# One wait of TensorE for free banks and for operands, where both stand on the same semaphore

## The reference

```python
x = x + attn(layernorm(x))            # Nystrom attention: 16 heads of 16, 64 landmarks
x = x + xattn(layernorm(x), ctx)      # cross attention to 64 masked keys of ctx, 16 heads
x = x + ffn(layernorm(x))             # per batch element one of 8 experts, chosen by the last row

# attn: q, k, v = split(x @ Wqkv + bqkv); q_l, k_l = means over 8 rows of q and k
a1, a2, a3 = softmax(q @ k_l), softmax(q_l @ k_l), softmax(q_l @ k)
out = a1 @ (pinv(a2) @ (a3 @ v)) @ Wout + bout
# pinv, six times: KV = a2 @ V; V = 0.25 * V @ (13 I - KV @ (15 I - KV @ (7 I - KV)))
# ffn: sel = argmax(gelu(last @ Wp1 + bp1) @ Wp2 + bp2)
# x + 0.3 * ((gelu(x @ W1[sel] + b1[sel]) @ W2[sel] + b2[sel]) @ Wo + bo)
```

## Time and profile before

| | us |
|---|---|
| median of 3 runs | 1419.36 |
| runs | 1419.16, 1419.36, 2244.75 |
| profiled execution, time | 1421.52 |
| profiled execution, span from first to last instruction | 1419.8 |

### The profile page before, as it was taken

How to read it: one execution, slowest core, us unless ns; L and a number is a source line. 1 busy time by engine, 2 the same in 40 slices (tenths; PEclk the granted TensorE clock), 3 DMA queues, 4 the chain that set the end, 5 groups by cost and what they waited for, 6 DMA issues and landing times.

```text
span 1419.8 us, 53827 instructions
## 1 busy us (share of the span) xinstructions
PE 1369.3 (96%) x23732; PEld 896.7 (63%) x23732; DVE 1032.9 (73%) x2194; ACT 666.6 (47%) x1230; POOL 569.9 (40%) x799
## 2 busy tenths in 40 slices
PE   6998999999999999999999999999999999999998
PEld 4756656655666666666666656666675656566555
DVE  2487877848677786867778686777878776898661
ACT  2423355354454545445454545545455453535652
POOL 6223444443615335361533526143352531516223
PEclk9999999999999999999999999999999999999999
DMA  8002010110101001010100101010010100001032
GB/s 281 1 3 91 5 62 3 44 66 11 57 12 51 19 30 39 3 57 12 50 19 19 51 3 57 12 51 18 15 55 4 51 3 19 18 4 37 3 97 64
DMA packets 40538, 53.19 MB, mean 37 GB/s; under 512 B 9699, under 2 KB 30451, under 8 KB 40307
## 3 DMA queue, kind: packets, MB, share of 16 engines
q1 hardware_dynamic: 31602, 41.37, 9.2%
q10 hardware_dynamic: 8704, 8.39, 1.7%
HBM read 37.16 MB, written 12.59 MB: 35 GB/s over the span
## 4 chain that ended last, share of the span: by engine, by line
PE 89%; DVE 4%; issue 2%; ACT 2%; DMA 1%; POOL 1%; DVEq 0%; SPq 0%; POOLq 0%; ACTq 0%
PE bank L1312 41%; PE bank L1555 8%; PE bank L1321 7%; PE bank L1331 7%; PE bank L1542 4%; PE bank L1381 2%; PE bank L1510 2%; PE bank L1446 2%; PE bank L1402 2%; PE bank L1435 2%; PE bank L1523 2%; PE bank L1369 1%; PE bank L1461 1%; PE bank L1408 1%; PE bank L1544 1%
## 5 line engine op out<-in xcount | busy, mean ns | idle before, releaser
L768 POOL TENSOR_TENSOR b<-ut,eye 128x256 f32<-128x256 f32 x192 | 137.2, 730 | 517.2 <-DVE ut L1151 445.2
L930 ACT ACTIVATE az<-bank 128x320 f32<-128x320 f32 x192 | 67.5, 400 | 191.6 <-PE bank L1321 191.2
L1208 DVE RECIPROCAL oT_x<-bank 128x256 f32<-128x256 f32 x64 | 109.3, 1734 | 22.5 <-PE bank L1555 22.5
L1312 PE MATMUL bank<-xnT_a,wqkv 128*128 128x512 f32 x256 | 123.6, 609 | 0.3 <-ACT xnT_a L854 0.3
L1312 PE MATMUL bank<-xnT_c,w1e 128*128 128x512 f32 x256 | 118.7, 605 | 3.0 <-DMA b1e<-in_b 3.0
L1208 DVE RECIPROCAL oT<-bank 128x256 f32<-128x256 f32 x64 | 111.5, 1747 | 10.4 <-PE bank L1555 10.3
L1312 PE MATMUL bank<-w2e,hT 128*128 128x256 f32 x512 | 117.3, 383 | 0.9 <-ACT hT L996 0.9
L1080 DVE TENSOR_REDUCE m<-bank 128x1 f32<-128x512 f32 x128 | 82.9, 680 | 39.4 <-PE bank L1402 37.9
L886 ACT ACTIVATE p3T<-bank 128x512 f32<-128x512 f32 x128 | 66.7, 604 | 83.4 <-PE bank L1435 83.4
L1312 PEld LDWEIGHTS bank<-w2e,hT 128*128 128x128 f32 x512 | 94.9, 190 | 15.2 <-issue 1.7
L1142 DVE SCALAR_TENSOR_TENSOR wb<-bank,eye 128x256 f32<-128x256 f32 x192 | 73.2, 411 | 33.0 <-PE bank L1321 32.3
(11 more groups left out here) (223 smaller groups left out, 3005.0 us busy)
## 6 DMA issues: line engine op xcount, KB each, us to landing
x_in<-in_x SPq DMA_DIRECT2D x16, 512.0 KB, 3.9
w1e<-in_W SPq DMA_DIRECT2D x16, 512.0 KB, 3.6
w2e<-w2o SPq DMA_DIRECT2D x16, 512.0 KB, 4.0
out<-base ACTq DMA_DIRECT2D x32, 256.0 KB, 2.2
row_e<-w2o_row SPq DMA_DIRECT2D x16, 128.0 KB, 4.5
hT<-in_W2T SPq DMA_DIRECT2D x2, 512.0 KB, 6.5
pT_x<-in_ctxT SPq DMA_DIRECT2D x1, 1024.0 KB
ctxT<-in_ctxT SPq DMA_DIRECT2D x16, 64.0 KB, 2.4
```

What stands on the lines that cost most here:

```text
L768: return g.tensor_tensor(b7[:, q, :], ut[:, q, :], eye[28 if it else 7][:].unsqueeze(1) .broadcast_to([P, 4, LM]), ALU.subtract).then_inc( ...
L1208: return v.reciprocal(oT[x][:, k, cols], tile(i, ("den" + x, k))[:, cols]).then_inc(dve_done, 1)
L1312: last = mm(dst, lhsT, rhs, start=(k == 0), stop=(k == len(pairs) - 1))
```

## The change

Where a step's wait for banks and its wait for operands stand on the same semaphore, they become one, for the higher of the two numbers. `body` now first takes the highest number per emptying engine into `emptied`, so that four banks emptied by DVE give one number. The new table `OPERANDS_FROM` says for each kind on which of the two semaphores its operands will be waited for anyway; only for the other one does `body` wait at its head. For the rest, `due` replaces `unmet` in the step's own branch: the number is the higher of the bank's and the operands'. In s3, t3, zT, a and o1 / ox the waits also change places, and iZ waits once for uz and ut together.

```diff
+OPERANDS_FROM = {"q": "A", "k": "A", "v": "A", "s3": "A", "x2T": "D", "mT3": "D", "t3": "AD", "zT": "AD", "z": "A",
+                 "a": "AD", "iT": "AD", "iZ": "AD", "jT": "AD", "jZ": "AD", "y": "D", "s1": "A", "sx": "A",
+                 "mT1": "D", "mTx": "D", "t1": "A", "tx": "A", "den1": "A", "denx": "A", "o1": "AD", "ox": "AD",
+                 "w1": "D", "wx": "D", "qx": "A", "gate": "A", "logit": "A", "h": "A", "y3": "A", "xnTc": "A"}
...
+        def due(eng, who, emptied, i, *steps):
+
+            n = max(emptied[who], *[DONE[who, i, s] for s in steps])
+            return n if first(eng, done[who], n) else 0
...
+                emptied = {"A": 0, "D": 0}
                 for j in range(banks_of(step)):
                     if BEFORE[i, step, j]:
                         who, i0, emptier = BEFORE[i, step, j]
-                        if c := unmet(pe, who, i0, emptier):
-                            pe.wait_ge(done[who], c)
+                        emptied[who] = max(emptied[who], DONE[who, i0, emptier])
+                if "D" not in OPERANDS_FROM.get(kind, ""):
+                    if first(pe, dve_done, emptied["D"]):
+                        pe.wait_ge(dve_done, emptied["D"])
+                if "A" not in OPERANDS_FROM.get(kind, ""):
+                    if first(pe, act_done, emptied["A"]):
+                        pe.wait_ge(act_done, emptied["A"])
...
                 elif kind == "t3":
                     if c := unmet(pe, "G", 0, ("cst",)):
                         pe.wait_ge(pool_done, c)
-                    if c := unmet(pe, "D", i, ("mT3",)):
-                        pe.wait_ge(dve_done, c)
                     if c := unmet(pe, "G", i, ("qbd",)):
                         pe.wait_ge(pool_done, c)
-                    if c := unmet(pe, "A", i, ("k", n)):
+                    if c := due(pe, "A", emptied, i, ("k", n)):
                         pe.wait_ge(act_done, c)
+                    if c := due(pe, "D", emptied, i, ("mT3",)):
+                        pe.wait_ge(dve_done, c)
...
                 elif kind == "zT":
-                    if c := unmet(pe, "A", i, *[("e3", n, j) for j in range(4)]):
+                    if c := due(pe, "D", emptied, i, ("v", 0), ("v", 1)):
+                        pe.wait_ge(dve_done, c)
+                    if c := due(pe, "A", emptied, i, *[("e3", n, j) for j in range(4)]):
                         pe.wait_ge(act_done, c)
-                    if c := unmet(pe, "D", i, ("v", 0), ("v", 1)):
-                        pe.wait_ge(dve_done, c)
...
                 elif kind in ("iT", "iZ"):
                     it = n
                     if it:
-                        if c := unmet(pe, "D", i, ("uz", it - 1, 0), ("uz", it - 1, 1)):
+                        if first(pe, act_done, emptied["A"]):
+                            pe.wait_ge(act_done, emptied["A"])
+                        ready = [("uz", it - 1, 0), ("uz", it - 1, 1)]
+                        if kind == "iZ":
+                            ready += [("ut", it - 1, 0), ("ut", it - 1, 1)]
+                        if c := due(pe, "D", emptied, i, *ready):
                             pe.wait_ge(dve_done, c)
                     else:
-                        if c := unmet(pe, "A", i, ("a", 0), ("a", 1)):
+                        if kind == "iZ":
+                            if c := due(pe, "D", emptied, i, ("z",)):
+                                pe.wait_ge(dve_done, c)
+                        elif first(pe, dve_done, emptied["D"]):
+                            pe.wait_ge(dve_done, emptied["D"])
+                        if c := due(pe, "A", emptied, i, ("a", 0), ("a", 1)):
                             pe.wait_ge(act_done, c)
...
                 elif kind in ("jT", "jZ"):
                     it = n
-                    if c := unmet(pe, "D", i, ("wb", it, 0), ("wb", it, 1)):
+                    if c := due(pe, "D", emptied, i, ("wb", it, 0), ("wb", it, 1)):
                         pe.wait_ge(dve_done, c)
-                    if c := unmet(pe, "A", i, ("az", it, 0), ("az", it, 1)):
+                    if c := due(pe, "A", emptied, i, ("az", it, 0), ("az", it, 1)):
                         pe.wait_ge(act_done, c)
```

More of the change, by code:

```diff
@@ L1363, in body @@
                     if i == 0:
-                        if c := unmet(pe, "D", 0, ("nmA",)):
+                        if c := due(pe, "D", emptied, 0, ("nmA",)):
                             pe.wait_ge(dve_done, c)
@@ L1388, in body @@
                 elif kind == "v":
-                    if c := unmet(pe, "A", i, ("xnTa", 0), ("xnTa", 1)):
+                    if c := due(pe, "A", emptied, i, ("xnTa", 0), ("xnTa", 1)):
                         pe.wait_ge(act_done, c)
@@ L1410, in body @@
                 elif kind == "x2T":
-                    if c := unmet(pe, "D", i, ("soft2",)):
+                    if c := due(pe, "D", emptied, i, ("soft2",)):
                         pe.wait_ge(dve_done, c)
@@ L1415, in body @@
                 elif kind == "mT3":
-                    if c := unmet(pe, "D", i, ("mp3",)):
+                    if c := due(pe, "D", emptied, i, ("mp3",)):
                         pe.wait_ge(dve_done, c)
@@ L1448, in body @@
                 elif kind == "z":
-                    if c := unmet(pe, "A", i, ("zT", 0), ("zT", 1)):
+                    if c := due(pe, "A", emptied, i, ("zT", 0), ("zT", 1)):
                         pe.wait_ge(act_done, c)
@@ L1453, in body @@
                 elif kind == "a":
-                    if c := unmet(pe, "A", i, ("x2T",)):
+                    if c := due(pe, "D", emptied, i, ("soft2",)):
+                        pe.wait_ge(dve_done, c)
+                    if c := due(pe, "A", emptied, i, ("x2T",)):
                         pe.wait_ge(act_done, c)
-                    if c := unmet(pe, "D", i, ("soft2",)):
-                        pe.wait_ge(dve_done, c)
                     for j in range(PAIRS):
@@ L1503, in body @@
                 elif kind == "s1":
-                    if c := unmet(pe, "A", i, ("q", n)):
+                    if c := due(pe, "A", emptied, i, ("q", n)):
                         pe.wait_ge(act_done, c)
@@ L1512, in body @@
                 elif kind == "sx":
-                    if c := unmet(pe, "A", i, ("qx", n)):
+                    if c := due(pe, "A", emptied, i, ("qx", n)):
                         pe.wait_ge(act_done, c)
@@ L1526, in body @@
                     x = kind[-1]
-                    if c := unmet(pe, "D", i, ("mp" + x,)):
+                    if c := due(pe, "D", emptied, i, ("mp" + x,)):
                         pe.wait_ge(dve_done, c)
@@ L1547, in body @@
                     x = kind[-1]
-                    if c := unmet(pe, "A", i, *[("e" + x, n, j) for j in range(4)]):
+                    if kind[0] == "o":
+                        if c := due(pe, "D", emptied, i, ("y",) if x == "1" else ("vx",)):
+                            pe.wait_ge(dve_done, c)
+                    if c := due(pe, "A", emptied, i, *[("e" + x, n, j) for j in range(4)]):
                         pe.wait_ge(act_done, c)
-                    if kind[0] == "o":
-                        if c := unmet(pe, "D", i, ("y",) if x == "1" else ("vx",)):
-                            pe.wait_ge(dve_done, c)
                     for j in range(4):
@@ L1557, in body @@
                     x = kind[-1]
-                    if c := unmet(pe, "D", i, ("o" + x, 0), ("o" + x, 1)):
+                    if c := due(pe, "D", emptied, i, ("o" + x, 0), ("o" + x, 1)):
                         pe.wait_ge(dve_done, c)
@@ L1565, in body @@
                 elif kind == "qx":
-                    if c := unmet(pe, "A", i, ("xnTb", 0), ("xnTb", 1)):
+                    if c := due(pe, "A", emptied, i, ("xnTb", 0), ("xnTb", 1)):
                         pe.wait_ge(act_done, c)
@@ L1569, in body @@
                 elif kind == "gate":
-                    if c := unmet(pe, "A", i, ("xnTc", 1)):
+                    if c := due(pe, "A", emptied, i, ("xnTc", 1)):
                         pe.wait_ge(act_done, c)
@@ L1573, in body @@
                 elif kind == "logit":
-                    if c := unmet(pe, "A", i, ("gate",)):
+                    if c := due(pe, "A", emptied, i, ("gate",)):
                         pe.wait_ge(act_done, c)
@@ L1577, in body @@
                 elif kind == "h":
-                    if c := unmet(pe, "A", i, ("xnTc", 0), ("xnTc", 1)):
+                    if c := due(pe, "A", emptied, i, ("xnTc", 0), ("xnTc", 1)):
                         pe.wait_ge(act_done, c)
@@ L1585, in body @@
                         pe.wait_ge(expert_out_loaded, 32 * (i + 1))
-                    if c := unmet(pe, "A", i, *[("h", f) for f in range(FM)]):
+                    if c := due(pe, "A", emptied, i, *[("h", f) for f in range(FM)]):
                         pe.wait_ge(act_done, c)
```

19 lines of the change are left out of this document (7 added, 12 removed).

## The result

The changed kernel takes 1401.22 us (median of 6 runs, 1396.81 to 1402.5), the kernel before 1419.26 us beside it. The two medians are 18 us or 1.3% apart; the ratio on record, of the fast runs alone (one of the six of the kernel before took 2244.75 us), is 0.9854, 95% interval 0.9838 to 0.9869, and so 1.5%. The profiled execution took 1401.27 us, its span is 1399.6 us against 1419.8.

A forecast was written before the change was run, and what follows sets the result against it. PE was taken as the bound, busy 1369.3 of 1419.8 us. Turns 4.1 to 6.2 us, ends 0.9 to 2.2, less 0.25, gave 4.7 to 8.1; 5.5 was taken off 1419.4, about 1414 us, range 1407 to 1420.4.

The forecast's parts named there:

- the seat of the late signal: Where a step's last signal is waited for: on the weight load, in the only EVENT_SEMAPHORE, or in the first of two.
- the three prices: Gain per late signal: only EVENT_SEMAPHORE to load 0.063 us, first of two to load 0.173, first of two to only 0.11.
- jT.2: Step jT of iteration 2: wb's late wait moves from the first of two EVENT_SEMAPHOREs to the load, 0.17 us a turn.
- jT.1: Step jT of iteration 1: wait from signal to load falls from 0.23 to 0.11 us, gaining 0.12 us a turn.
- iT.5: Step iT of iteration 5: one EVENT_SEMAPHORE stays; 0.11 us less, of which matmuls ahead leave 0.055 us a turn.
- w1.0: Step w1.0: oT's late wait moves from the only EVENT_SEMAPHORE to the load, 0.007 to 0.063 us a turn.
- zT.1: Step zT.1: p3T's late signal costs 0.063 us less, of which 0.002 to 0.063 us a turn shows.
- tx.0: Step tx.0: vt's late signal costs 0.173 us less, but s1's matmuls ahead leave only 0.005 to 0.091 us.
- (a): Rival: DVE or ACT backlog swallows the gain, 0 to 2 us, about 1418.5 us; chance 0.17 together with (d).
- (b): Rival: PE's sequencer is the bound; 355 fewer EVENT_SEMAPHOREs free 39 us, 1380 us, or weaker 1411; chance 0.07.
- (c): Rival: late signals move off the load into remaining EVENT_SEMAPHOREs, 0.063 us each, up to 5.8 us slower, 1425; chance 0.04.
- (d): Rival: the build packs waits otherwise, EVENT_SEMAPHOREs stay near 808, time 1419.4 us; chance 0.17 together with (a).

The follow-up runs named there:

- e9: Kernel before with nothing merged; only each step's waits reordered, the one whose signal comes last listed first, on the weight load: 1407.76 us, ratio 0.9892.
- e4: Changed kernel with a satisfied wait listed first in every step that waits, so every real wait goes into an EVENT_SEMAPHORE: 1424.12 us, ratio 1.0011.
- e1: Changed kernel padded with satisfied waits behind the real ones until every step has its old number of EVENT_SEMAPHOREs, 808 in all: 1406.26 us, ratio 0.9880.
- e6: Changed kernel with each step's waits reordered, the one whose signal came last in its trace listed first, on the load: 1398.06 us, ratio 0.9841.
- e8: e4 with 128 more EVENT_SEMAPHOREs of satisfied waits ahead of the first matmul: 1426.81 us, ratio 1.0048.
- e10: e6 with 128 more EVENT_SEMAPHOREs of satisfied waits ahead of the first matmul: 1411.46 us, ratio 0.9922.
- e11: e6 run again, unaltered: 1397.83 us, ratio 0.9825.
- e5: The changed kernel run once more, unaltered: 1400.41 us, ratio 0.9866.

## Why the prediction was wrong

**What was right.** The count, 355 EVENT_SEMAPHOREs to go and 453 to stay. The mechanism, the seat of the late signal, and the three prices: e9 and e4 show that order alone gives three quarters of the gain (0.0108 of 0.0146), and takes all of it. The middle's idle time fell by 4.8 us, "some 4" in the prediction. The sign, and that it stays within 2%. The single steps: jT.2 0.22 us a turn by the medians (forecast 0.17), jT.1 0.12 (0.12), iT.5 0.054 (0.055), w1.0 0.07 (0.007 to 0.063), zT.1 0.09 (0.002 to 0.063, so above it).

**The term that was mis-sized: tx.0's bound.** "0.005 (the shortest distance that this pair of steps ever has)" to 0.091; it gave 0.19, above the upper bound too. In the kernel before vt's signal was late and seated in the first of two in 10 of 16 batches, all those of the middle, so the pair's shortest distance was itself a delayed one. A floor read from instances that all suffer the same delay is not a floor. With this step and the smaller excesses a turn gives 0.68 us at steps without an edge, where 0.41 to 0.62 was forecast: 6.8 us for ten turns.

**The step that failed: a late signal was priced by the three latencies from signal to load (0.063, 0.173 and 0.11 us) and by nothing else.** The sum has no term for what else stands behind a held sequencer, the fetch of the next block. That is 0.24 us a turn (0.52 against 0.28), in single steps such as iZ.0 of batch 11 (1.01 us) and iT.0 of batch 7 (0.71). At the ends, where the forecast had single steps at 0.063 or 0.173 us, `a` of batch 1 gives 1.06, t3.1 of batch 2 2.5 and iT.5 of batch 15 1.2. The other half of the sentence, that an EVENT_SEMAPHORE whose signal is old costs nothing, held nearly: e1's 355 cost at most 4 to 5 us together.

The 20.2 us between the two spans divide, as an estimate from these readings, into 7.7 us of pauses (10.1 less 2.4), 1.5 us of the wait for b1e (2.49 less 0.99, below), 1.6 us in steps that touch the lower clock in one of the two profiles, and so some 9.4 us for the waits themselves, where 4.7 to 8.1 were forecast. The row "[0.79 <-issue]" above and others like it were in the trace of before; "issue" had 2% of the chain, 28 us, and I asked nothing of it.

Is it shown that a late signal in an EVENT_SEMAPHORE makes the fetch late? In the middle turns, yes by experiment. The cleanest pair is the kernel before and e9, with the same 808 EVENT_SEMAPHOREs and only the order changed. The others agree: with no late signal on the load the edges cost 1.12 us a turn (e4), with all of them there 0.04 (e6); with the edges moved by 128 instructions the pauses remain in the one and remain absent in the other (e8, e10), and e9 loses its middle pauses. The packets themselves say it too: asked for over 3 us after the previous edge are 13 blocks in the kernel before, 19 and 20 in e4 and e8, and 2, 3, 4 and 4 in e6, e11, e10 and e9, of some 187 each. At the ends it is not the only cause. t3.1 of batch 2 pauses 1.9 us in e9 as well, whose late signals are on the load; the block was asked for 3.8 us after the previous edge. The DMA view of e9 from 188 to 196 us, slices of 0.2 us:

```profile
DMA  0156243324799999999999999999999775520000
```

The DMA engines are at 0.9 and more from 190.2 to 194.2 us, and the block was asked for at 192.6. That a fetch asked for beside large stores also comes late fits this, and perhaps e10's 2.8 us pause, whose transfers are not shown here; no run here takes those transfers away, so it stays open.

**A third part, at the start.** PE in the kernel before, batch 1's h.3, and the same in the changed kernel:

```profile
288.45 1.06 PE L1523 MATMUL bank<-kx_bd,qxT 32*128 32x128 f32 x32
...
292.00 5.37 PE L1312 MATMUL bank<-xnT_c,w1e 128*128 128x512 f32 x8 [2.49 <-DMA b1e<-in_b]
```

```profile
283.48 1.06 PE L1543 MATMUL bank<-kx_bd,qxT 32*128 32x128 f32 x32
...
285.53 3.67 PE L1322 MATMUL bank<-xnT_c,w1e 128*128 128x512 f32 x8 [0.99 <-DVE m_x L1192]
```

Before, PE waits 2.49 us for the load of b1e, and the eight matmuls of h.3 and h.0 take 5.37 us; changed it waits 0.99 us for DVE, and they take 3.67. The table of stretches of the kernel before, columns as in the earlier trace rows, at the two places where the granted clock fell (PEclk, behind POOL's count; the last 2.5 us apart):

```profile
1174.00:1181.00 7.00, 7.00 (x102) 4.16 (x100) 3.41 (x9) 1.16 (x2) 0.00 (x0) 0.54 0.00 0
293.00:297.00 4.00, 4.00 (x7) 1.67 (x6) 2.89 (x13) 0.69 (x1) 0.47 (x2) 0.58 0.03 9
```

0.58 and 0.54 are mostly the 1.2 GHz level; the one at 293 us begins 1 us after the 2.49 us in which PE waited for b1e. Together h.3 and h.0 are 3.2 us shorter in the changed kernel. Why b1e comes last in the one and not in the other was not tried. The forecast took a granted clock of 0.99 to 1.00 from stretches of 280 us and more; those at the lower level are too short to show there. In the changed kernel they fell in other places from one profile to the next (above, at e5), and no run here isolates them; the 1.7 us by which the eight matmuls above differ is what one such place cost.

**The rivals.** (a), swallowed: the gain is larger than its own terms. (b), the sequencer is the bound: its price, 0.11 us for each of 355, is refuted by e1 and e9, but its marker, a turn under 82.4, came true, and its subject was half right: the sequencer matters through what it has not yet passed. The Trainium skill ("TensorE: Matmul & The Clock Gate", table at its top) gives PE a queue of 64 entries with weight loads pulled ahead, from which I had concluded that short instructions are hidden; e1, 4 to 5 us for 355 of them, agrees with that nearly, as long as the sequencer is not held. (c), late signals that move off the load: its mechanism is real, as e4 shows with +22 us against the changed kernel, though 4 steps did it in the change, as I had counted. Counted step by step, 141 signals that no matmul ahead covers at 0.063 us each, e4 would have lost 9 us against the changed kernel; it lost 22; the edges, 0.84 us a turn more than in the changed kernel and 12.4 us of pauses more in all, are most of the rest, and its 640 further EVENT_SEMAPHOREs may be some of it. (d) is refuted by the count.

## What to carry to other kernels

List first, in each step, the wait whose signal comes last, so that it rides on the first weight load; which one that is stands in the trace, and it is worth more than the number of waits (16.5 us with none dropped, 2 us more on top of the merging). When a sequencer-held wait is priced, look beyond the step at what the sequencer has not yet passed, first of all the next block of instructions: list the pauses inside steps that have no wait ("<-issue") and see whether they stand at a fixed distance in the instruction stream. Take no floor from instances that all carry the delay which the change removes. And where each execution has its mean granted clock, compare the kernels at equal clock too (here 17 us at 0.996).

## What was not expected of the hardware

- PE's instructions come in blocks of 256 (16 KB packets on queue q8); the edge is never passed sooner than 1.20 us after the packet landed (14 profiles; the shortest is 1.20 to 1.35 us in each), a packet takes 1.0 to 1.1 us (median), and the pauses go from 0.2 to 2.8 us.
- The latency from signal to load depends on the place within an EVENT_SEMAPHORE of two waits: over the profiles 42 ns on the load, 105 alone in the last EVENT_SEMAPHORE or as w3 or w4 beside w2, but 60 as w2 itself where it shares that EVENT_SEMAPHORE (shortest tenth of some 130 steps of e4), 215 in the first of two. e4's wb at jT.2 sat at 60, which is one reason why its waits gave back 0.29 us of a turn and not more.
- 128 satisfied EVENT_SEMAPHOREs ahead of all work moved the first weight load by 7.6 us (11.9 to 19.5 from e4 to e8), 59 ns each.
